# A graph layer's setup on one core: the branch decided early, 20-byte records, and the first tiles begun inside the setup

## The reference: what is computed

```python
edge_index = jnp.stack([src, dst])
h = jnp.maximum(_layernorm(x, axis=-1), 0.0)
# layer 0: x @ W_S.T + b ; sum over edges of exp(-w) * (x[dst] @ W_N.T + b) into row src; relu
x = x + _L0_gnn_ref(h, edge_index, edge_weight, ...)
h = jnp.maximum(_layernorm(x, axis=-1), 0.0)
# layer 1: softmax over each node's incoming edges of q[dst].k[src], sum of v[src], skip, elu
x = x + _L1_gnn_ref(h, edge_index, ...)
```

## Time and profile before

| what | value |
|---|---|
| three runs | median 868.57 us (866.88 to 869.34) |
| the profiled execution | 869.26 us, of which the span of recorded work is 867.5 us |
| PE busy in the span | 756.2 us (87%) |
| DVE busy | 754.6 us (87%) |
| ACT busy | 510.7 us (59%) |
| POOL busy | 256.3 us (30%) |
| granted TensorE clock, mean | 0.974 of full speed |

### The profile page before, as it was taken

The page is one execution under the profiler, slowest core; times in us unless marked ns, Lnnn a source line. Parts: engine busy times, 40 slices in busy tenths (PEclk is TensorE's granted clock), DMA queues, the critical chain, the costliest instruction groups (busy, mean ns, idle before and its releaser), DMA issues.

```text
span 867.5 us, 22993 instructions
## 1 busy us (share of the span) xinstructions
PE 756.2 (87%) x8799; PEld 654.9 (75%) x8846; DVE 754.6 (87%) x908; ACT 510.7 (59%) x1034; POOL 256.3 (30%) x199
## 2 busy tenths in 40 slices
PE   0064799999999999999999787799999999999996
PEld 0052677777777777777777466699999999999996
DVE  6647999999999999999996556799999999999982
ACT  5954667667676776767766243344554555455444
POOL 5640000000000000000000230366667667666766
PEclk9997899999999999999999799699999999999999
DMA  9540113123132131221312441204244334423400
GB/s 232 142 135 2 78 78 147 81 83 144 76 132 94 76 151 76 123 104 76 151 76 113 163 180 61 92 1 155 86 154 157 124 113 156 157 94 142 157 7 11
DMA packets 17516, 94.96 MB, mean 109 GB/s; under 512 B 2594, under 2 KB 8844, under 8 KB 10956
## 3 DMA queue, kind: packets, MB, share of 16 engines
q1 hardware_dynamic: 14428, 89.18, 27.0%
q0 software_dynamic: 3056, 5.35, 2.7%
HBM read 50.31 MB, written 44.21 MB: 109 GB/s over the span
## 4 chain that ended last, share of the span: by engine, by line
PE 59%; DVE 11%; issue 11%; POOL 4%; ACT 2%; DMA 2%; DVEq 1%; SPq 0%; POOLq 0%; ACTq 0%
PE bank L1041 14%; PE bank L1182 13%; PE bank L1192 12%; DVE oh_key L873 6%; PE bank L1031 5%; PE bank L1103 5%; PE bank L1101 5%; POOL sm L458 3%; DVE kT L777 3%; DMA gl_sb<-gt 2%; PE bank L1145 1%; PE bank L1179 1%; PE bank L1150 1%; DVE mx L960 1%; DVE oh_lo L870 1%
## 5 line engine op out<-in xcount | busy, mean ns | idle before, releaser
L458 POOL TENSOR_TENSOR sm<-sm,mbc 128x896 f32<-128x896 f32 (+1 forms) x100 | 186.3, 1896 | 74.1 <-ACT mbc L647 74.1
L1101 PE MATMUL bank<-oh_key,oh_lo 128*128 128x100 bf16 x1600 | 172.2, 209 | 13.5 <-DVE oh_key L873 11.8
L1041 PE MATMUL bank<-wsb,hvb 128*128 128x512 f32 (+1 forms) x350 | 166.2, 580 | 13.7 <-DVE kT L777 12.4
L1182 PE MATMUL bank<-qT,kT 128*128 (+1 forms) x1250 | 167.9, 279 | 7.3 <-issue 3.9
L1103 PE MATMUL bank<-oh_key,oh_lo 128*128 128x50 bf16 x3200 | 172.5, 187 | 0.0
L1101 PEld LDWEIGHTS bank<-oh_key,oh_lo 128*128 128x128 bf16 x1600 | 156.3, 98 | 19.6 <-DVE oh_key L873 12.4
L1182 PEld LDWEIGHTS bank<-qT,kT 128*128 128x128 f32 x1250 | 163.7, 196 | 5.0 <-DVEq L173 1.2
L1103 PEld LDWEIGHTS bank<-oh_key,oh_lo 128*128 128x128 bf16 x3200 | 165.5, 98 | 1.1
L554 ACT COPY wsb<-bank 128x512 f32<-128x512 f32 (+1 forms) x175 | 88.1, 553 | 106.3 <-PE bank L1031 106.3
L1192 PE MATMUL bank<-vals,sm 128*128 128x129 f32 x1250 | 147.5, 274 | 0.2 <-ACT sm L651 0.2
L960 DVE TENSOR_REDUCE mx<-sm 128x128 f32<-128x3200 f32 x25 | 146.2, 5847 | 0.9
(11 more groups left out here) (120 smaller groups left out, 707.1 us busy)
## 6 DMA issues: line engine op xcount, KB each, us to landing
gt<-gst SPq DMA_DIRECT2D x25, 1600.0 KB, 5.6
gl_sb<-gt SPq DMA_DIRECT2D x25, 1600.0 KB, 6.8
records<-rec SPq DMA_DIRECT2D x1, 1612.0 KB
out<-res SPq DMA_DIRECT2D x24, 64.0 KB, 1.6
dst_i<-in_dst SPq DMA_DIRECT2D x1, 403.0 KB, 5.7
dstn_i<-in_dst_next SPq DMA_DIRECT2D x1, 403.0 KB, 6.6
src_i<-in_src SPq DMA_DIRECT2D x1, 403.0 KB, 7.2
w_in<-in_edge_weight SPq DMA_DIRECT2D x1, 403.0 KB, 7.8
```

The costliest lines, as they stand in the source:

```text
L458: pool.tensor_tensor(part, part, mbc[:, v % 2:v % 2 + 1, :].to_broadcast([P, n, P]), ALU.subtract).then_inc(sub_done, 1)
L1041: T.matmul(ps(6 + at)[:, 0:n], hvb[:, w, :], wsb[:, at, 0:n], start=True, stop=True).then_inc(l0_mm, 1)
L1101: T.matmul(cells, lo, oh_key[:, u, m, 0:2 * KEYS, i], start=True, stop=False, skip_group_check=True)
L1182: ins = T.matmul(score_bank(g)[:, j * P:(j + 1) * P], kT[:, (a + j) * P:(a + j + 1) * P], qT[:, bass.ds(t * P, P)], start=g < LIFT, stop=T ...
```

## The change

It makes five edits.
1. **The test for the usual path moves to the input.** The host lays out a third copy of `dst`, shifted by 128 edges (`dst_far`). Sortedness is `dst[i+1] < dst[i]`, overflow is `dst[i+128] <= dst[i] | 1`. DVE makes both (L790, L791), ACT sums each over its row, PE over the partitions, DVE writes `flag` in the middle of stage 1. There is no `end_stage(…, 1)`; each engine branches when its own stream gets there.
2. **`If(fast)` comes first** in each stream and the slow path stands behind it, in `Else`, with a barrier of its own (`start_slow`).
3. **Records are five fp32 words** (20 bytes: key, low part, three weight parts). The key `NT*dst + hi` is made once per edge. A window has 128 records. The bf16 fields are the upper halves of fp32 words, which PE reads in place; `open_windows` is one subtraction.
4. **Stage 1's tail goes into the usual path.** The last features, windows, neighbour and self products are issued by PE and ACT between the groups of tile 0 and 1. DVE starts quad 0 once the first fetched group is turned.
5. Eight of the 25 tiles' statistics move from ACT to DVE (`bn_stats`), the bias of `hv` from DVE to POOL (behind the window fetches), the two small tables ahead of the layer norm on ACT.

```diff
-            sp.wait_ge(s_recst, 32)
...
-            slow = sp.value_load(flag[0:1, 0:1], min_val=0, max_val=1)
-            end_stage(sp, 1)
+            fast = sp.value_load(flag[0:1, 0:1], min_val=0, max_val=1)
...
+            with pool.If(fast):
+                pool.wait_ge(s_recst, 32)
+                for g, (a, n) in enumerate(WG):
+                    pool.wait_ge(s_start, g + 1)
+                    for k in range(a, a + n):
+                        pool.indirect_dma_start(win[:, k, :], None, records,
+                                                bass.IndirectOffsetOnAxis(start_i[:, k:k + 1], 0)).then_inc(s_win[g], 16)
+                neighbour_features()
...
-            nc.scalar.copy(rec[:, :, R_LO], src_lo[:]).then_inc(s_rec, 1)
-            nc.scalar.activation(rec[:, :, R_HI], src_hi[:], ACT.Identity, bias=1.0).then_inc(s_rec, 1)
+            nc.scalar.copy(rec[:, :, W_LO], src_lo[:]).then_inc(s_rec, 1)
+            for k in range(2):
+                act.wait_ge(s_part, 2 * k + 1)
+                nc.scalar.copy(rec[:, :, W_W + k], part_b[:, k, :]).then_inc(s_rec, 1)
...
+            for k in range(2):
+                act.wait_ge(s_badt, k + 1)
+                nc.scalar.activation(bad_e[:, k, :], bad_e[:, k, :], ACT.Identity, accum_out=bad[:, k:k + 1]).then_inc(s_bad, 1)
...
+                        if isinstance(t, int) and t == 0 and j == 3:
+                            act_neighbours(4, len(TG))
+                            take_windows(1, 3)
+                        if isinstance(t, int) and t == 0 and j == 7:
+                            act_self(0, 4)
+                            take_windows(3, 5)
+                        if isinstance(t, int) and t == 1 and j == 1:
+                            act_self(4, NPC)
+                            act.wait_ge(s_hvb, len(TG))
...
+                act_features(0, 3)
+                take_windows(0, 1)
+                act_features(3, len(TG) + 1)
+                act_neighbours(0, 4)
+                act_tile(0, 0, 0, False)
...
-                step(V.tensor_tensor(ahead[:, blocks, :], win32[:, blocks, 0:SLOTS, 0],
-                                     nid[:, blocks].unsqueeze(2).to_broadcast([P, n, SLOTS]), ALU.subtract))
-                V.scalar_tensor_tensor(out=over[:, blocks], in0=win32[:, blocks, SLOTS, 0], scalar=-1.0, in1=nid[:, blocks],
-                                       op0=ALU.add, op1=ALU.is_le).then_inc(s_over, 1)
-                V.scalar_tensor_tensor(out=xin_field(F_KEY)[:, blocks], in0=ahead[:, blocks, :], scalar=float(NT),
-                                       in1=win_field(R_HI)[:, blocks], op0=ALU.mult, op1=ALU.add).then_inc(s_xin, 1)
-                for f, cell in ((F_LO, R_LO), (F_W, R_W), (F_W + 1, R_W + 1), (F_W + 2, R_W + 2)):
-                    V.tensor_copy(xin_field(f)[:, blocks], win_field(cell)[:, blocks]).then_inc(s_xin, 1)
+                V.tensor_tensor(xin[:, blocks, :], win32[:, blocks, :, W_KEY],
+                                nid[:, 1, blocks].unsqueeze(2).to_broadcast([P, n, SLOTS]), ALU.subtract).then_inc(s_xin, 1)
...
+                open_windows(0)
+                dve.wait_ge(s_tab, 2)
+                dve.wait_ge(s_xtev, 1)
+                quad(0, 0, 0, [], [])
+                open_windows(1)
+                open_windows(2)
+                quad(0, 0, 1, [], [])
+                open_windows(3)
+                open_windows(4)
+                dve_tile(1, 1, False)
+                dve.wait_ge(s_xtev, NB)
+                dve.wait_ge(acc_ev, NPC)
...
+                        if isinstance(t, int) and t == 0 and j == 2:
+                            pe_neighbours(4, len(TG))
+                            turn_windows(1, 3)
+                        if isinstance(t, int) and t == 0 and j == 6:
+                            pe_self(0, 4)
+                            turn_windows(3, 5)
+                        if isinstance(t, int) and t == 1 and j == 0:
+                            pe_self(4, NPC)
+                            pe.wait_ge(acc_ev, NPC)
+                            pe.wait_ge(s_xtev, NB)
```

More of the change, by code:

```diff
@@ L535, in _, with copy_turned @@
-            for j, (a, k) in enumerate(PC):
-                act.wait_ge(acc_mm, j + 1)
-                nc.scalar.activation(kT[:, a * P:(a + k) * P], ps(6 + j % 2)[:, 0:k * P], ACT.Identity,
-                                     bias=bcol[:, 0:1]).then_inc(acc_ev, 1)
-            take_windows(WG[EARLY:])
-            act.wait_ge(s_flag, 1)
-            slow = act.value_load(flag[0:1, 0:1], min_val=0, max_val=1)
-            end_stage(act, 1)
+            def copy_turned(n):
+                a, k = TG[n]
+                act.wait_ge(s_tp, n + 1)
+                nc.scalar.copy(hT[:, a * P:(a + k) * P], ps(n % 2)[:, 0:k * P]).then_inc(s_hT, 1)
@@ new lines, in act_self, with take_windows @@
+            def act_self(from_, to):
+                for j in range(from_, to):
+                    a, k = PC[j]
+                    act.wait_ge(acc_mm, j + 1)
+                    nc.scalar.activation(kT[:, a * P:(a + k) * P], ps(6 + j % 2)[:, 0:k * P], ACT.Identity,
+                                         bias=bcol[:, 0:1]).then_inc(acc_ev, 1)
+            def take_windows(from_, to):
+                for b in range(WG[from_][0], sum(WG[to - 1])):
+                    act.wait_ge(s_xt, b + 1)
+                    nc.scalar.copy(xt[:, :, b * P:(b + 1) * P],
+                                   ps(4 + b % 2).bitcast(BF16)[:, 0:FIELDS * P].rearrange("p (f n) -> p f n", f=FIELDS)
+                                   ).then_inc(s_xtev, 1)
@@ new lines, in _ @@
+            V.tensor_scalar(minus_b[:], ctab[:, P:2 * P], -1.0, None, ALU.mult).then_inc(s_id, 1)
+            dve.wait_ge(s_sum, LN_ACT)
+            V.tensor_scalar(nmean[:, 0:LN_ACT], nmean[:, 0:LN_ACT], -1.0 / D, None, ALU.mult).then_inc(s_ln, 1)
+            count_chunks(0)
+            dve.wait_ge(s_badsum, 1)
+            V.tensor_scalar(flag[:], ps(6)[0:1, 0:1], 0.5, None, ALU.is_lt).then_inc(s_flag, 1)
+            dve.wait_ge(s_x, 32)
+            for t in range(LN_DVE):
+                last = V.bn_stats(ln_st[:, t, :], xs[:, LN_ACT + t, :])
@@ new lines, in _ @@
+            step(last)
+            for t in range(LN_DVE):
+                last = V.bn_aggr(ln_mv[:, t, :], ln_st[:, t, :])
+            step(last)
+            V.tensor_scalar(nmean[:, LN_ACT:], ln_mv[:, :, 0], -1.0, None, ALU.mult).then_inc(s_lnd, 1)
+            V.tensor_scalar(rstd[:, LN_ACT:], ln_mv[:, :, 1], float(D), None, ALU.mult).then_inc(s_lnd, 1)
+            count_chunks(1)
+            count_chunks(2)
+            dve.wait_ge(s_std, 1)
+            V.reciprocal(mean[:], rstd[:]).then_inc(s_ln, 1)
@@ L1017, in _ @@
-            pe.wait_ge(s_flag, 1)
-            slow = pe.value_load(flag[0:1, 0:1], min_val=0, max_val=1)
-            end_stage(pe, 1)
+            pe.wait_ge(s_bad, 2)
+            pe.wait_ge(s_init, 5)
+            for k in range(2):
+                ins = T.matmul(ps(6)[0:1, 0:1], bad[:, k:k + 1], ones[:, 0:1], start=k == 0, stop=k == 1)
+            ins.then_inc(s_badsum, 1)
+            pe.wait_ge(s_flag, 1)
+            fast = pe.value_load(flag[0:1, 0:1], min_val=0, max_val=1)
+            pe.wait_ge(s_id, 3)
```

597 lines of the change are left out of this document (310 added, 287 removed).

## The result

| | before | changed |
|---|---|---|
| median of the timed runs | 868.03 us (866.88 to 869.34, 4 runs) | 854.73 us (853.25 to 858.59, 4 runs) |
| profiled execution; its span | 869.26; 867.5 us | 856.0; 854.2 us |
| quad 4's key block starts | 106.68 | 91.04 |
| granted TensorE clock, mean | 0.974 | 0.983 |

The ratio is 0.9845, 95% interval 0.9825 to 0.9864: shorter by 1.6%, with 1 well outside the interval, and 3.7 us above the forecast of 851. Each set of a kernel has its own runs of the kernel before beside it, so I compare the ratios.

A forecast was written before the change was run, and what follows sets the result against it. The start of quad 4, ahead of the full loop, was taken to decide: 106.7 to 88.0 gains 18.7, the branch costs 1.0, so 869.26 − 18.7 + 1.0 = 851.6 profiled, 851 as median; range 844 to 859.

The forecast's parts named there:

- What bounds the kernel: PE and DVE fill the tile loop; gain lies ahead, in when quad 4 starts, from which the loop repeats itself.
- Rival 6: Longer instruction streams make the tile loop's backward jump wait on each of 11 turns; 870 to 885; chance 0.04.
- Up to the features: Stage 1 on ACT, loads through layer-norm statistics: features start at 36.0, only 4 us earlier.
- the flag: Stage 1: DVE's flag comes 1.4 us after the two new row sums on ACT, at 27.5.
- The start of the fetches: POOL's window fetches start at 31.4, after flag and its load of 3.2 us; 13 fetches last to 47.5.
- From 36.0 to quad 4: ACT is the thread: 43.2 us of work plus 7.0 of waits, so quad 4 at 86.2 at full clock.
- the checkpoints: Between features and quad 4: window 0 turned 43, first one-hot 44, first group 55, group 4 66, group 8 77.
- it waits where PE's step is longer than its own: 7.0: ACT's waits for PE between features and quad 4, at windows, neighbour and self products, groups and turns: 7.0 us.
- The clock: PE's bursts from 37 to 86: half clock adds 7, a quarter taken, +1.8, so quad 4 at 88.0.
- Rival 2: PE at half clock through the mixed tiles: quad 4 at 92 to 94, 855 to 859; chance 0.20.
- The branch: Each engine's jump over the slow path on leaving stage 2 costs 1.0 us, between 0.3 and 3.2.
- Rival 3: POOL's bias additions and DVE's weighted one-hots block each other; with slow strided weight loads 859 to 863; chance 0.08.

The follow-up runs named there:

- gather_late: Against the changed kernel, POOL fetches window groups 1 to 4 only once ACT has taken windows 0 and 1; 855.98 us, ratio 0.9856.
- after_again: The changed kernel run once more, unchanged, on chip B; 848.89 us, ratio 0.9784.
- relus_only: Against the changed kernel, ACT does the last four relu groups before the first window copies, PE's slow path left behind; 850.41 us, ratio 0.9806.
- relus_in_gap: Against the changed kernel, PE's slow path ahead and ACT's last four relu groups before windows 0 and 1; 847.17 us, ratio 0.9771.
- pe_slow_ahead: Against the changed kernel, PE's stream alone has the slow path ahead of the usual one; chip A, 853.58 us, ratio 0.9815.
- pe_slow_again: The kernel of pe_slow_ahead unchanged, run once more on chip C; 847.22 us, ratio 0.9755.
- barrier: Against the changed kernel, a drain and a meeting of all five engines ahead of the branch; 854.29 us, ratio 0.9854.

## Why the prediction was right, and where its steps missed

**What bounds the kernel** held: only the start of quad 4 moved, and what follows moved with it. 106.68 to 91.04 is 15.64; of it the span kept 13.3 (867.5 to 854.2). From quad 4 to DVE's last `bn_aggr` of stage 2 both kernels take 379.39 us (to 486.07 and 470.43). From there to ACT's `ln_c` it is 4.89 before and 6.39 after, 1.5 lost; the other 0.8 goes later. In the loop a tile takes 15.59 (107.00 to 122.59), the forecast 31.2 for two. Rival 6 is out: the jump back in the loop costs nothing new.

In the forecast's terms, quad 4 came 3.0 us late and the way out of stage 2 cost 0.5 more than its 1.0; with the 0.8 that is the 4.4 us between 851.6 and the 856.0 of the profiled execution.

**Up to the features** the steps held to 0.4 us on the changed kernel's own trace (36.0 forecast, 35.57), and the flag to 0.04. The start of the fetches came out nearly right by another path. The forecast has POOL wait for the flag and its load, which by its own terms is 27.5 + 3.2 = 30.7 and not 31.4, with the records landed before, at 29. In the trace POOL waits last for the records' landing, until 30.75. No engine waited for a window group there. POOL's fetches of destinations before it took at most 1.63 us, where with the longer record casts they had taken up to 3.40.

**From 36.0 to quad 4** the sum has two outcomes. Without the hold the checkpoints window 0 at 43 and first one-hot at 44 were 41.98 and 42.76, and quad 4 was 85.49 against 88.0. Of these 2.5 us, 1.0 is the features' earlier start (35.03); from the features to quad 4 it was 50.46 against 52.0, so this term was 1.5 too large; some 0.8 of it is the clock (1.8 forecast, about 1 measured, below). With the hold they were 47.82, 48.60 and 91.04, and this term, 55.47, was 3.5 too small. The step that failed is "it waits where PE's step is longer than its own: 7.0": a wait of 6.58 us for work that is already done was not in it, although shows 3.0 `<-remote` at L519. I had read that row as a cost of PE's step. That the traces with and without the hold divide by chip (or by batch) is shown by twelve traces: held in 4 of 4 on chip A, in 0 of 7 on B and 0 of 1 on C, with one kernel on A and on C. That it goes with the fetches' traffic rests on chip A alone: in gather_late it moved when they moved.

**The clock** term of +1.8 is a quarter of 7, but the words before it, 12 × 0.46 "and as much again", make 11. It was not spent in the first trace (1.00 from 40 to 123). Elsewhere it was. after_again first, relus_only below it, in the same columns as the earlier trace rows:

```profile
58.00:62.00 4.00, 3.53 (x55) 3.50 (x56) 1.31 (x2) 3.25 (x8) 4.00 (x4) 0.71 0.00 0
62.00:66.00 4.00, 3.14 (x30) 2.89 (x30) 4.00 (x2) 2.79 (x6) 3.62 (x2) 0.86 0.01 2
```

```profile
58.00:62.00 4.00, 4.00 (x70) 3.93 (x68) 4.00 (x3) 3.51 (x9) 3.95 (x2) 1.00 0.00 0
62.00:66.00 4.00, 2.24 (x27) 1.59 (x24) 4.00 (x4) 3.99 (x8) 4.00 (x3) 1.00 0.03 6
```

4 × 0.29 and 4 × 0.14 are 1.7 us of lost clock, so 3.4 us at the lower level, 1.2 GHz. relus_in_gap had the same (0.69 and 0.89) and relus_only not; with features 0.2 apart their quads 4 are 85.27 and 84.13. Such a stretch costs about 1 us. Rival 2, half clock throughout, did not happen on any chip.

**The branch** is the mis-sized term: "I take 1.0, nearer the 0.53". PE idled 3.35, 2.82 and 3.40 us before stage 3 with the jump (the changed kernel's first trace, after_again, relus_only), and 0.76, 0.75 and 0.76 without it (pe_slow_ahead, pe_slow_again, relus_in_gap). So the jump cost 2.1 to 2.6, between the 1.0 and the upper bound of 3.2. By the ratios, taking it away brought 2.6 us (0.9845 and 0.9815), 2.5 (0.9784 and 0.9755) and 3.0 (0.9806 and 0.9771). Only the last pair has intervals apart, and only it is of one chip; the three agree. The net of 1.5 in the first trace is luck of the clock. PE's last product began 2.72 us after DVE's last `bn_aggr` there, at a granted clock of 0.96 in 471 to 474, and 3.48 before the change, at 0.69 in 486 to 490. In after_again, at 0.60, the net is 2.3. The transfers of instructions in 473 to 478 of the changed kernel, and in 472 to 478 of pe_slow_ahead:

```profile
q8 instruction: 2, 0.03, 2.7%
```

```profile
q8 instruction: 1, 0.02, 1.0%
```

With the jump, one transfer of q8 begins inside the gap (in 474.0 to 474.5, it takes 1.1 us) and a second follows the gap (477.0 to 477.5). Without the jump there is one, in 474.5 to 475.0, when stage 3 has begun (473.93). The other two pairs show the same. The Trainium skill (Runtime: NRT & Kernel Launch, Instruction fetch mechanics) states that a taken branch out of the loaded pages waits for a fetch. By that rule the traces agree, though the transfer is over at least 1 us before the gap is, and which engine q8 serves isn't shown. They give the price: 2.1 to 2.6 us on PE, and none that is seen on ACT, whose table load began 0.41 us after its last copy. At the entry, PE's jump costs nothing, as it has some 8 us to wait there (27.5 to 35.57): with it, in pe_slow_ahead, its first transposes come 1.70 us after the features start, as without it (37.27 and 35.57).

**Rival 3** was real, and free in the changed kernel. POOL's bias addition took 4.27 us at 59.41 where I had 1.1, while DVE wrote one-hots; in after_again four took 10.13. ACT never waited for `hvb`. That the pair can hold DVE for longer shows in barrier (8.21 us).

**Altogether** 851 lay between two sizes: 854.73 with a hold of 5 to 6 us that was not in the sum, 848.89 without. That the first median lies so near the forecast is in part luck: the hold was not foreseen, and a clock that stayed at full speed and features 0.4 us early paid some of it back. That it lies within the range, up to 859, is owed to the width, which was set for a slower clock.

What single edits are worth on chip B at quad 4: no meeting before the branch 3.6 us, the mixing 3.9, the statistics 1.8, or some 3.4 with the 1.6 of the clock (one execution each). That is about half of the 21.2 us between 106.68 and 85.49, which also contains the hold in the trace of the kernel before. The shifted destinations, the fp32 records and DVE's early quads were not undone one by one; how they share the rest stays open.

A version below both kernels is the changed one with PE's slow path ahead: 847.22, ratio 0.9755. Against the first set of the changed kernel (0.9845) the intervals are apart, against the second (0.9784) they still touch; the pair relus_only and relus_in_gap settles that this edit gains.

## What to carry to other kernels

Put the usual path where the jump falls into a wait, engine by engine: on the engine that everyone waits for at the exit the long alternative belongs ahead, if that engine is idle at the entry. Here the cost was seen on PE alone; DVE's, POOL's and SP's jumps were not measured. When steps are mixed to fill gaps, sum the engine that threads through them; what mixing brings is only its waits. Before explaining a wait by a kernel's order, run the same kernel again: a wait for work that is already recorded as done needs another cause than the order of the program, and an edit that seems to cure it may only have run on another chip.

## What the runs showed of the hardware

- On chip A, and in the first traces of both kernels, ACT went on 4 to 6 us after the recorded end of the matmuls it waited for, late in a burst of 13 window fetches (241 GB/s in 40 to 50 of the changed kernel's trace), and on chips B and C not, with the same bursts. It cost 5 to 6 us (848.89 and 854.73; 847.22 and 853.58). In gather_late the recorded matmuls of PE stood 0.7 to 1.4 us apart meanwhile. What differs between the chips is open. The recording is under suspicion, as every execution here was recorded, and the six traces with a hold are short of records: they hold 1531 to 1648 landings of transfers, the eight without one 1952 to 1967, and for four of the six the view has no time to landing for the window fetches, which for all others is 3.6 to 4.1 us. The Trainium skill (NOTIFIC — the notification-queue block, Overflow: three behaviours, one of which stalls the engine) states that full record queues can be set to stall their producer; no run here shows that.
- The jump over its slow path cost PE 2.1 to 2.6 us at the end of stage 2, in three pairs of traces.
- A fetch's descriptor work on POOL takes 0.95 us; beside DVE's one-hots up to 6.31 (barrier, 55.14 to 61.45). DVE's `xin` subtraction took 8.21 us beside POOL's bias additions (barrier).
